# Summing the expert parts on GpSimd instead of TensorE, in a kernel of two attention blocks, a mixture of experts and a top-32 attention

## What is computed

```
x = x + attention_A(layernorm(x), ctx)      # 16 heads of 8, softmax over 77 keys, with a key mask
x = x + ffn_A(layernorm(x))                 # attention over the 4 batch rows, layernorm (y1), then
                                            #   y2 = layernorm(y1 + moe(y1)): 8 experts, top-1 gate, capacity 256
x = x + attention_B(layernorm(x), ctx)      # 16 heads; only the 32 largest of 77 scores enter the softmax
x = x + ffn_B(layernorm(x))                 # r * ((relu(k))^2 @ W_v), with the row before mixed in
```

## Time and profile before

| | us |
|---|---|
| median of three runs | 580.47 |
| lowest, highest | 578.23, 587.06 |
| the profiled execution, its own time | 588.05 |
| its span, from the first instruction to the last | 586.2 |
| TensorE busy | 505.3 (86%) |
| VectorE busy | 482.3 (82%) |
| ScalarE busy | 290.8 (50%) |
| GpSimd busy | 278.9 (48%) |
| mean granted TensorE clock | 0.819 of 2.4 GHz |

### The profile page before, as it was taken

The page is one execution under the profiler, slowest core; times in us unless marked ns, Lnnn a source line. Parts: engine busy times, 40 slices in busy tenths (PEclk is TensorE's granted clock), DMA queues, the critical chain, the costliest instruction groups (busy, mean ns, idle before and its releaser), DMA issues.

```text
span 586.2 us, 11489 instructions
## 1 busy us (share of the span) xinstructions
PE 505.3 (86%) x2929; PEld 374.3 (64%) x2929; DVE 482.3 (82%) x3014; ACT 290.8 (50%) x797; POOL 278.9 (48%) x400
## 2 busy tenths in 40 slices
PE   5989997797996998699988898899889878798887
PEld 4569766466765864467665666667667556676665
DVE  5844678939678698987949789999999999999971
ACT  1224542223243425320585668787876687745431
POOL 4501041504226346741455656875775668645511
PEclk9979996967797579855595988898888979769885
DMA  8500000000000000000000000000000000000000
GB/s 293 246 0 1 2 1 1 1 1 1 2 1 1 1 2 1 0 2 1 2 6 5 2 5 2 7 7 1 7 6 5 2 7 6 2 11 6 1 6 9
DMA packets 5935, 9.64 MB, mean 16 GB/s; under 512 B 744, under 2 KB 4976, under 8 KB 5616
## 3 DMA queue, kind: packets, MB, share of 16 engines
q1 hardware_dynamic: 5584, 8.35, 4.0%
q10 hardware_dynamic: 288, 0.56, 0.3%
HBM read 7.86 MB, written 1.05 MB: 15 GB/s over the span
## 4 chain that ended last, share of the span: by engine, by line
PE 43%; DVE 38%; ACT 7%; issue 6%; POOL 4%; DMA 1%; SPq 0%; DVEq 0%; ACTq 0%; POOLq 0%
DVE area_b L956 15%; DVE top L948 14%; PE psT L1320 8%; PE psM L1091 5%; PE psM L1288 3%; PE psM L1228 2%; PE psM L1236 2%; PE psS L1059 2%; PE psM L1034 2%; PE psT L1080 2%; PE psS L1062 2%; PE psM L1129 2%; PE psM L1223 1%; PE psM L1164 1%; DVE mx L715 1%
## 5 line engine op out<-in xcount | busy, mean ns | idle before, releaser
L1320 PE MATMUL psT<-mrow,mones 65*128 65x308 bf16 x608 | 118.2, 347 | 2.0 <-ACT vv L671 1.2
L948 DVE MAX8 top<-area_b 128x8 f32<-128x77 f32 x768 | 112.7, 226 | 0.0
L956 DVE MATCH_REPLACE8 area_b<-top,area_b 128x77 f32<-128x77 f32 x512 | 107.0, 226 | 0.0
L1320 PEld LDWEIGHTS psT<-mrow,mones 65*128 65x128 bf16 x608 | 68.5, 114 | 40.7 <-issue 14.1
L1091 PE MATMUL psM<-vblk,pT 128*128 128x81 f32 (+1 forms) x320 | 48.9, 319 | 9.4 <-ACT early L568 4.5
L1091 PEld LDWEIGHTS psM<-vblk,pT 128*128 128x128 f32 (+1 forms) x320 | 47.0, 234 | 12.8 <-issue 11.1
L956 DVE MATCH_REPLACE8 area_b<-top,area_a 128x77 f32<-128x77 f32 x256 | 53.6, 225 | 0.0
L1272 PE MATMUL psT<-consts,p 128*128 128x128 f32 (+1 forms) x160 | 35.4, 351 | 12.9 <-POOL p L433 8.2
L587 ACT ACTIVATE mparts<-psM,cur 128x128 f32<-128x128 f32 x128 | 38.0, 367 | 16.4 <-PE psM L1228 16.1
L1288 PEld LDWEIGHTS psM<-vblk,pT 128*128 128x128 f32 (+1 forms) x320 | 42.0, 212 | 6.4 <-issue 5.7
L1288 PE MATMUL psM<-vblk,pT 128*128 128x81 f32 (+1 forms) x320 | 43.5, 295 | 2.3 <-ACT pT L641 1.9
(11 more groups left out here) (222 smaller groups left out, 1085.1 us busy)
## 6 DMA issues: line engine op xcount, KB each, us to landing
area_a<-in_w1T SPq DMA_DIRECT2D x1, 2064.0 KB, 11.6
area_b<-in_w SPq DMA_DIRECT2D x1, 2048.0 KB, 17.0
x<-in_x SPq DMA_DIRECT2D x4, 256.0 KB, 6.6
out<-fin SPq DMA_DIRECT2D x16, 64.0 KB, 1.6
rows<-in_rows SPq DMA_DIRECT2D x1, 576.0 KB, 6.8
vblk<-in_vblk SPq DMA_DIRECT2D x1, 540.0 KB, 16.6
weights<-in_weights SPq DMA_DIRECT2D x1, 516.0 KB, 7.1
consts<-in_consts ACTq DMA_DIRECT2D x1, 392.5 KB, 4.0
```

The lines of the kernel that those rows point to most:

```text
L948: ins = e.max(tops[:, r, h], (left if r else scores_sb[t % RING])[:, h])
L956: ins = e.match_replace(left[:, h], tops[:, r, h], (left if r else scores_sb[t % RING])[:, h], GONE)
L1320: mm(bank[:, 0:B * KEYS], mones[:], mrow.rearrange("p b k -> p (b k)"), start=True, stop=True)
```

## The change

1. `total` moves from TensorE to GpSimd: the gated products are added in place as a tree of five `tensor_tensor` and written to a new tile `msum` in SBUF, from where `sum2`, `square2` and `norm2` now read. With that, `m0_free` waits for `mb_out` (the last gated product taken out) instead of `n2_out`.
2. `FILLS` = 0: no fillers.
3. `mrow` and `mones`, the operands of the mask product, have 128 rows instead of 65. The further rows of `mrow` are zero.
4. The value products stream 3, 3, 4, 4 and six times 5 copies in their ten matmuls, 44 in place of 30, with up to 135 columns each.
5. `ORDER` is new. All 1794 steps other than the fillers are the same in number and name; on VectorE the sequence is 93% the same, on TensorE 68%, on GpSimd 73%, on ScalarE 63% (the likeness of the two lists without fillers, by a comparison of sequences, with `total` in both).

```diff
-COPIES = 3
-FILLS = 304
+FILLS = 0
+BANK = 512
+def copies(c):
+    at = FIRST[c] * VE
+    return next((n, (BANK - at) // n) for n in (5, 4, 3) if (BANK - at) // n >= VW - at)
...
-        mrow = sb("mrow", [65, B, KEYS], BF16)
-        mones = sb("mones", [65, P], BF16)
+        mrow = sb("mrow", [P, B, KEYS], BF16)
+        mones = sb("mones", [P, P], BF16)
...
-            hold(e, s["n2_out"], begun(step, "turn"))
+            hold(e, s["mb_out"], 3 * begun(step, "turn"))
...
+                def total():
+                    hold(e, s["mb_out"], 3 * t + 3)
+                    e.tensor_tensor(mparts[:, 0:4], mparts[:, 0:4], mparts[:, 4:8], ALU.add).then_inc(s["e_step"], 1)
+                    e.tensor_tensor(mparts[:, E], mparts[:, E], cur[:, 0:D], ALU.add).then_inc(s["e_step"], 1)
+                    hold(e, s["e_step"], 4 * t + 1)
+                    e.tensor_tensor(mparts[:, 0:2], mparts[:, 0:2], mparts[:, 2:4], ALU.add).then_inc(s["e_step"], 1)
+                    hold(e, s["e_step"], 4 * t + 3)
+                    e.tensor_tensor(mparts[:, 0], mparts[:, 0], mparts[:, 1], ALU.add).then_inc(s["e_step"], 1)
+                    hold(e, s["e_step"], 4 * t + 4)
+                    hold(e, s["n2_out"], t)
+                    e.tensor_tensor(msum[:], mparts[:, 0], mparts[:, E], ALU.add).then_inc(s["mty"], 1)
...
-                sum2, square2, norm2 = ln_passes(0, t, psM0[:, 0:D], lambda: hold(e, s["mty"], t + 1), s["n2_neg"], s["n2_sq"],
+                sum2, square2, norm2 = ln_passes(0, t, msum[:], lambda: hold(e, s["mty"], t + 1), s["n2_neg"], s["n2_sq"],
...
-                            ins = mm(pvs0[:, :, FIRST[c] * VE:FIRST[c] * VE + VB], pT[0:w, c],
-                                     vblk0[0:w, b, c, None, :].broadcast_to([w, COPIES, VB]), start=(c == 0),
+                            ins = mm(streams(psM0, c), pT[0:w, c],
+                                     vblk0[0:w, b, c, None, :].broadcast_to([w, copies(c)[0], VB]), start=(c == 0),
...
-                def total():
-                    hold(e, s["mb_out"], 3 * t + 3)
-                    mm(psM0[:, 0:D], ident, cur[:, 0:D], start=True, stop=False)
-                    for x_ in range(E + 1):
-                        ins = mm(psM0[:, 0:D], ident, mparts[:, x_], start=False, stop=(x_ == E))
-                    ins.then_inc(s["mty"], 1)
```

More of the change, by code:

```diff
@@ new lines @@
+max21@2 norm4@0 load@4 scale2@3 max22@2 fturn@0 shift@0 turn@4 max23@2 norm2@3 up@0 mark20@2 copy2@1 affine@3 copy@4 mark21@2 moe0@4
+acts@0 mark22@2 sum3@3 half@0 square3@3 down@0 mark23@2 fvalue@0 value@1 scale3@3 gated0@4 max30@2 end@0 max31@2 norm3@3 max32@2
+max33@2 lturn@3 moe1@4 norm@1 lT@3 cut@2 ask@3 gated1@4 qT@3 moe2@4 add3@1 scores@3 gated2@4 sum4@1 total@4 square4@1 keep@3 sign@2
+max00@3 max01@3 max02@3 scale4@1 max03@3 sum2@4 mark00@3 square2@4 keys@4 norm4@1 load@5 mark01@3 dif@3 fturn@1 shift@1 turn@5
@@ new lines @@
+mark02@3 copy@5 up@1 mark03@3 moe0@5 product@2 max10@3 acts@1 max11@3 down@1 fvalue@1 max12@3 gated0@5 max13@3 mark10@3 turn0@2
+scale2@4 exp@3 mark11@3 moe1@5 half@1 norm2@4 mark12@3 affine@4 copy0@2 gated1@5 mark13@3 turn1@2 end@1 max20@3 sum3@4 moe2@5
+square3@4 max21@3 copy1@2 scale3@4 max22@3 gated2@5 turn2@2 max23@3 norm3@4 total@5 mark20@3 copy2@2 lturn@4 mark21@3 value@2 lT@4
+mark22@3 mark23@3 max30@3 sum2@5 load@6 ask@4 norm@2 qT@4 turn@6 square2@5 max31@3 scores@4 add3@2 copy@6 max32@3 scale2@5 sum4@2
@@ new lines @@
+moe0@6 max33@3 square4@2 keep@4 keys@5 scale4@2 norm2@5 max00@4 gated0@6 cut@3 max01@4 norm4@2 max02@4 moe1@6 max03@4 fturn@2
+shift@2 mark00@4 affine@5 sign@3 up@2 mark01@4 dif@4 mark02@4 mark03@4 acts@2 max10@4 product@3 sum3@5 down@2 square3@5 max11@4
+fvalue@2 gated1@6 max12@4 max13@4 mark10@4 moe2@6 exp@4 scale3@5 turn0@3 mark11@4 mark12@4 half@2 norm3@5 end@2 gated2@6 lturn@5
+copy0@3 mark13@4 lT@5 total@6 turn1@3 max20@4 ask@5 copy1@3 max21@4 qT@5 max22@4 turn2@3 scores@5 copy2@3 max23@4 value@3 mark20@4
@@ new lines @@
+value@6 gated1@10 max00@8 cut@7 max01@8 max02@8 max03@8 lturn@9 mark00@8 down@5 lT@9 dif@8 moe2@10 gated2@10 ask@9 mark01@8 fvalue@5
+qT@9 sign@7 scores@9 norm@6 mark02@8 add3@6 total@10 mark03@8 sum4@6 max10@8 square4@6 max11@8 keep@9 max12@8 max13@8 mark10@8
+product@7 sum2@10 mark11@8 square2@10 mark12@8 mark13@8 scale4@6 exp@8 turn0@7 max20@8 max21@8 scale2@10 copy0@7 max22@8 norm4@6
+turn1@7 max23@8 load@11 norm2@10 end@5 fturn@6 turn@11 shift@6 mark20@8 copy@11 affine@10 up@6 mark21@8 copy1@7 mark22@8 keys@10
@@ new lines @@
+turn2@7 acts@6 moe0@11 mark23@8 sum3@10 half@6 square3@10 down@6 copy2@7 max30@8 scale3@10 gated0@11 max31@8 value@7 max32@8
+norm3@10 max33@8 fvalue@6 end@6 max00@9 max01@9 cut@8 lturn@10 moe1@11 max02@9 lT@10 max03@9 ask@10 norm@7 gated1@11 mark00@9 add3@7
+qT@10 dif@9 moe2@11 sum4@7 mark01@9 scores@10 gated2@11 sign@8 mark02@9 mark03@9 total@11 max10@9 keep@10 max11@9 max12@9 square4@7
+max13@9 mark10@9 product@8 mark11@9 sum2@11 square2@11 mark12@9 mark13@9 max20@9 load@12 exp@9 turn@12 scale2@11 max21@9 turn0@8
@@ L1470 @@
+turn0@15 part2@15 add3@14 copy0@15 part3@15 sum4@14 turn1@15 square4@14 value0@15 scale4@14 copy1@15 turn2@15 norm4@14 value1@15
+copy2@15 fturn@14 shift@14 value2@15 up@14 norm@15 close@15 acts@14 root@15 down@14 half@14 fvalue@14 closen@15 end@14 fturn@15
+shift@15 up@15 acts@15 half@15 down@15 end@15""".split()
 def kernel(**inputs):
```

233 lines of the change are left out of this document (97 added, 136 removed).

## The result

The changed kernel takes 580.11 us (median of 20 executions, 574.57 to 586.83), the kernel before 583.8 us in as many beside it. The ratio is 0.9935, with a 95% interval from 0.9906 to 0.9964: 0.6% faster, which is within the 2% that count as no change. 562 us was predicted, in a range of 547 to 578. The profiled execution of after has a span of 578.4 us, that of before 586.2, so the two profiles differ by 7.8. The medians differ by 3.7 only: the profiled execution of before (588.05 us) was 4.3 above its median, that of after (580.24) at its own. So about half of the 7.8 may belong to that one execution of before, whose trace is the only one that I have of it; the gains that are read from the two traces are to be taken with this.

The account below looks back on a forecast made before the run. VectorE was taken as the bound from 350 to 560 us, not before 350 or at the end. -16 - 5 - 4 + 2 + 0 = -23 from 588.05 gave 565; carrying 3 us over gave 562, range 547 to 578.

Parts of the forecast that it names:

- I price this stretch at nothing: From 350 to 560 us: VectorE stays the bound, GpSimd reaches 176.5 of 210 us, so no gain or loss.
- three signs of being wrong: Clock under 0.8 in the first 220 us; VectorE waiting for scores after 350; its two-SBUF-tensor products stretching beside trees.
- Fillers of 65 rows don't buy it: From 245 to 292 us TensorE was 99% busy yet at half clock, so fillers don't buy clock; argued against slowdown.
- that rule as a rival: First 220 us: the clock falls without fillers and the stretch gets longer, 582 to 595 us; chance 0.10.
- -16 and -5: -16 us of VectorE idle from 220 to 350 us with fillers out; -5 us in the first 220 us.
- the stall: First 220 us: a value product's 4.50 us wait for tile 0's `norm2` goes, with 5.1 us of VectorE idle.
- third rival: First 220 us: denser value products bring the clock back sooner, 11 us on the path, 551 us; chance 0.27.
- The loop is shorter by 3 us: Tile to tile: the next `turn` waits some 4 us for tree and `load`, not 7.0, so scores keep up.
- second rival: GpSimd's queue: the tree waits behind `cut` and `product`, so the gain is lost, 577 us; chance 0.20.
- Contention, 2 us: Trees of tiles 0 to 3 beside VectorE products, and queueing of `total@2`: +2 us; contention bounds nothing to 14.4.
- The end, -4: Last stretch: 12 fillers leave the chain and the last value product goes ahead of `up@14`; bounds -1.4 and -5.
- Masks at nothing: Mask matmuls with 128 rows keep their 308 columns, so they cost nothing.

Follow-up runs that it names:

- e10: The changed kernel with four of the tree's five additions left out, so the sum of the experts is not computed: 576.97 us, ratio 1.0073.
- e1: The kernel before with its 304 fill entries taken out and nothing else changed: 592.01 us, ratio 1.0178.
- e9: The kernel before with the denser value products and without any fillers, old order and identity matmuls kept: 581.39 us, ratio 0.9996.
- e7: The kernel before with the denser value products alone, fillers and old order kept: 570.18 us, ratio 0.9859.
- e8: The changed kernel with 168 fillers (336 matmuls of 128 rows) put back behind tile 5's search: 587.02 us, ratio 1.0159.
- e11: The kernel before with the denser value products and without the 98 filler matmuls from 245 to 292 us: 568.31 us, ratio 0.9826.
- e12: The kernel before with GpSimd's tree in place of the identity matmuls alone, fillers and old order kept: 633.21 us, ratio 1.0949.
- e15: The changed kernel with masks and ones of 65 rows, as before the change: 584.83 us, ratio 1.0151.
- e17: The kernel before with the denser value products and 128 rows in the masks and so in its 608 filler matmuls: 557.78 us, ratio 0.9647.

## Why the prediction was wrong

**What bounds the kernel: half right.** The reading of the earlier trace rows, that VectorE has idle time to give up to 350 us and none from there to 560, stood. The step that failed follows it: "I price this stretch at nothing. The cover is GpSimd's remaining 16%". I named the wrong cover. GpSimd had 152.2 us of 210, less than the 176.5 I had counted, and its share was not the limit: with a tree of 0.5 us it had 130.4, and VectorE waited no less (e10). In the old order, what hid TensorE's part of each tile behind VectorE was TensorE's clock of 0.87, and 298 of the 608 filler matmuls stand in that stretch. I asked what the clock would do without fillers, but only for the first 220 us, where it even rose, from 0.84 to 0.87. After 220 it fell from 0.74 to 0.61, and from 350 on from 0.87 to 0.68. e1 measures the term that I put at nothing: 11.6 us from tile 5 to 15, e9 against e7 9.0 us. After gives back 6.6 in the same place. That this is the same term is likely, but not shown, since e8 had fillers and the higher clock and gave back as much.

Of the sum, -23 was predicted and -7.8 came, 15.2 us less: 6.6 by this step, 4.6 at the end, 4.0 up to tile 5. None of the three signs of being wrong that I had named came: the clock in the first 220 us was 0.87, VectorE waited for no scores behind 350, and its busy time hardly grew. The wait that came, for value products, was not on my list.

**"Fillers of 65 rows don't buy it": false.** I took it from one spell, 245 to 292 us, in which TensorE was busy with fillers at half clock. That shows that fillers did not lift the clock there, not that they hold it nowhere else. By the Trainium skill, "TensorE: Matmul & The Clock Gate", Part 1, activity releases the clock and gaps take it back. After 350 us this case agrees (0.87 with fillers, 0.73 without, in e1); from 245 to 292 us, at half clock and 99% busy, it does not. I had that rule as a rival and put its price into the wrong stretch.

**Up to tile 5: right in sign, too large, and for the wrong reason.** Predicted were -16 and -5 from the fillers, the stall and the loop, measured 15.0 us. e7 gets 17.1 without touching a filler, e1 only 8.3 by taking all out, e11 nothing more by taking out those of the spell. The spell at half clock came to an end with the denser value products, which I had priced at nothing and kept as the third rival. That rival had the mechanism (half-clock time goes) but set it in the first 220 us, at 11 us on the path: in e7 VectorE is busy 4.6 us more there and 12.1 more from 220 to 350. In after, 6.6 us of what was won by tile 5 went again later on.

**The tree: its time right, its place wrong.** The sum predicted 3.4 us. The groups of GpSimd in after, over the whole run, make 1.27 + 0.77 + 0.50 + 0.50 + 0.455 = 3.5 us a tile:

```profile
L412 POOL TENSOR_TENSOR mparts<-mparts 128x512 f32<-128x512 f32 x16 | 20.3, 1269 | 3.7 <-ACT mparts L611 3.6
L415 POOL TENSOR_TENSOR mparts<-mparts 128x256 f32<-128x256 f32 x16 | 12.4, 774 | 0.0
L417 POOL TENSOR_TENSOR mparts<-mparts 128x128 f32<-128x128 f32 x16 | 8.0, 501 | 1.3
L420 POOL TENSOR_TENSOR msum<-mparts 128x128 f32<-128x128 f32 x16 | 8.0, 498 | 1.3
L413 POOL TENSOR_TENSOR mparts<-mparts,cur 128x128 f32<-128x128 f32 x16 | 7.3, 455 | 0.0
```

"The loop is shorter by 3 us" failed. In the kernel before with the tree alone the loop was longer by 4.5 us a tile (44.9 over ten, e12). I counted waits on the path from tile to tile and none of what stands behind the tree in GpSimd's and ScalarE's order. The second rival had that queue, at 577 us: the nearest of the numbers. That was luck: its mechanism is not what held after back, since a tree of 0.5 us gains 0.5% in it at most (e10).

**Contention, 2 us:** VectorE's busy time rose by 1.6 us in all (482.3 to 483.8 by the pages), of the size that I took, and far from the upper bound of 14.4.

**The end, -4:** +0.6. The 12 fillers at the end are gone, but VectorE waits as long as before: 3.2 and 3.5 us for the last two value products, 3.3 for `vv` and 2.4 ahead of `p` (L995), where before it was 7.0 for the last value product and 5.6 for `vv`. The clock is at 0.5, 0.5 and 0.8 in the last three slices, before at 0.8, 0.8 and 0.5. **Masks at nothing:** right for after as far as measured (e15 is unclear). The same rows in fillers are not nothing (e17).

**The whole change on one ladder:** no fillers +1.8%, tree in the old order +5.8%, denser products -1.3%, the new order with the masks -6.5% (5.9% by the times). The order repays the tree and little more; the gain of the denser products pays for the fillers.

## What to carry to other kernels

- An engine that is 99% busy in a stretch is the bound there only as long as the others keep their pace. Before pricing a change at nothing in such a stretch, ask what the change does to the speed of the engine that feeds it, its clock above all, and price the next wait.
- Filler work has to be judged in each stretch on its own, by a run without it. With 128 rows in fillers and masks the kernel was 2.6% faster here than with 65 in the same places.
- Work moved to another engine is priced by what stands behind it in the queues that it enters, not by its duration: 3.5 us a tile cost 5.8% in the old list without fillers, 9.5% in it with them, and 0.5% at most in the new one.

## What the runs showed of the hardware

- How busy TensorE was did not tell its granted clock. From 245 to 292 us it was busy 46.8 of 47 us at 0.50, 43.2 us at 0.85 in e7 and 40.1 us at 0.96 in e17. There the three differ in the columns of the value products (81 before, up to 135 in e7 and e17), in the rows of fillers and masks (65, 65, 128), and, since two of them are ahead, in the steps that fall into the stretch. That 63 more rows, nearly all of them in instructions which nobody waits for, are worth 2.6% was the surprise of this study.
- More columns in a value product cost next to nothing: 339 ns for 135 columns and 350 for 81 in after, 350 to 560 us, at a clock of 0.68; 319 and 309 in e7, at 0.89.
- GpSimd's load did not touch MAX8: in after, the 537 of 1024 that ran inside a `tensor_tensor` of GpSimd took 223 ns on average, those outside any took 223 too.
